# A morphological dilation with seven row sides in PSUM, their ends merged into the pair tiles

## The reference, cut to what matters

```python
pad = jnp.pad(u, ((0, 0), (0, 0), (r, r), (r, r)), constant_values=NEG)   # r = 5
def body(acc, idx):                       # idx = 0 .. 120: 11 rows di x 11 columns dj
    sl = dynamic_slice(pad, (0, 0, di, dj), (Bn, C, H, W))
    acc = maximum(acc, sl - kflat[:, idx][None, :, None, None])
```

## Time and profile before

| what | value |
|---|---|
| median of 3 runs (lowest to highest) | 10253.23 us (10250.52 to 10257.87) |
| the profiled execution: its time, and its span in the trace | 10254.56 us, 10252.8 us |
| DVE, ACT, POOL, PE busy over the span | 97%, 90%, 87%, 84% |
| DMA issued by POOL (queue q0), share of the 16 engines | 60.9% |

### The profile page before, as it was taken

The page is one execution under the profiler, slowest core; times in us unless marked ns, Lnnn a source line. Parts: engine busy times, 40 slices in busy tenths (PEclk is TensorE's granted clock), DMA queues, the critical chain, the costliest instruction groups (busy, mean ns, idle before and its releaser), DMA issues. The chain is left out here.

```text
span 10252.8 us, 72623 instructions
## 1 busy us (share of the span) xinstructions
PE 8565.8 (84%) x18068; PEld 3322.9 (32%) x18068; DVE 9963.9 (97%) x5623; ACT 9179.9 (90%) x6861; POOL 8875.6 (87%) x3274
## 2 busy tenths in 40 slices
PE   2888888888888888888888888888888887998899
PEld 0333333333333333333333333333333333443333
DVE  8999999999999999999999999999999999999999
ACT  2999999999999999999999999999999997888776
POOL 2889888898988999898988888898889887777998
PEclk9999999999999999999999999999999999999999
DMA  8788878888888888888888888888888876444776
GB/s 322 149 157 151 155 155 159 158 160 158 159 157 159 159 158 159 153 159 156 160 155 156 159 158 160 159 158 157 160 159 158 158 141 137 178 182 187 268 282 258
DMA packets 442070, 1751.43 MB, mean 171 GB/s; under 512 B 23888, under 2 KB 130384, under 8 KB 392784
## 3 DMA queue, kind: packets, MB, share of 16 engines
q0 software_dynamic: 278528, 1110.51, 60.9%
q1 hardware_dynamic: 163152, 636.41, 16.6%
HBM read 391.58 MB, written 201.33 MB: 58 GB/s over the span
## 5 line engine op out<-in xcount | busy, mean ns | idle before, releaser
L589 PE MATMUL chain<-dx,mats 128*128 128x512 f32 x10240 | 4979.5, 632 | 940.6 <-ACT chain L639 940.3
L530 POOL TENSOR_TENSOR m<-m,u 128x2048 f32<-128x2048 f32 x1024 | 4338.1, 4350 | 187.1 <-ACT m L621 185.9
L589 PEld LDWEIGHTS chain<-dx,mats 128*128 128x128 f32 x10240 | 1917.0, 197 | 4002.9 <-ACT chain L639 2095.8
L718 DVE SCALAR_TENSOR_TENSOR acc_a<-m,kt,acc_a 128x2048 f32<-128x2048 f32 x1344 | 3162.5, 2353 | 38.2 <-issue 2.4
L639 ACT ACTIVATE chain<-chain,gap_r 128x1024 f32<-128x1024 f32 x2560 | 2694.2, 1086 | 232.2 <-PE chain L589 230.5
L718 DVE SCALAR_TENSOR_TENSOR acc_a<-t,kt,acc_a 128x2048 f32<-128x2048 f32 x1024 | 2411.9, 2355 | 34.2
L501 POOL DMA_DIRECT2D t<-u x1024 | 1486.4, 1563 | 652.8 <-ACT t L621 635.1
L526 POOL TENSOR_TENSOR m<-u,m 128x2048 f32<-128x2048 f32 x384 | 1707.1, 4445 | 0.0
L621 ACT ACTIVATE t<-dx,gap_l 128x2048 f32<-128x2048 f32 x768 | 1540.5, 2006 | 0.4 <-issue 0.4
L589 PE MATMUL chain<-u,mats 128*128 128x512 f32 x3072 | 1456.0, 605 | 71.8 <-ACT chain L639 71.8
L718 DVE SCALAR_TENSOR_TENSOR acc_a<-u,kt,acc_a 128x2048 f32<-128x2048 f32 x576 | 1357.0, 2356 | 20.5
(11 more groups left out here) (149 smaller groups left out, 6876.4 us busy)
## 6 DMA issues: line engine op xcount, KB each, us to landing
t<-u POOLq DMA_DIRECT2D x1024, 1059.0 KB, 8.7
u<-x_dram SPq DMA_DIRECT2D x32, 2688.0 KB, 30.6
xt<-x_dram SPq DMA_DIRECT2D x32, 2048.0 KB, 14.2
x_scratch<-x SPq DMA_DIRECT2D x64, 1024.0 KB, 10.7
h_scratch<-h SPq DMA_DIRECT2D x32, 2048.0 KB, 7.2
both<-h_scratch SPq DMA_DIRECT2D x64, 1024.0 KB, 9.3
out_dram<-res SPq DMA_DIRECT2D x64, 1024.0 KB, 4.9
both<-x_scratch SPq DMA_DIRECT2D x28, 2304.0 KB, 12.6
```

The lines of the kernel that those rows point to most:

```text
L530: nc.gpsimd.tensor_tensor(m_tile(j), m_tile(j), rows, ALU.add).then_inc(m_ready, 1)
L589: added = nc.tensor.matmul(chain[h][:, r:r + 2, :], weight, src[:, top:top + 2, dj:dj + W], start=False, stop=True, skip_group_check=True)
L718: nc.vector.scalar_tensor_tensor(out=acc_a[:], in0=src, scalar=k_base, in1=acc_a[:], op0=ALU.subtract, op1=ALU.max).then_inc(a_done, 1)
```

## The change

Seven row sides are folded in PSUM instead of six. The five right ones of the old list stop a step earlier (4 instead of 5), and the two taps left over become a pair; the new seventh side has 5 steps. So the steps stay at 29 for each half, and the ends that VectorE reads rise from 12 to 14 halves. A finished half is no longer merged into a second accumulator but into half of a pair tile that waits for its own merge (`chain_targets`: the second `m` or `t` tile behind it in the DVE order), with a scalar that is the difference of the two weights (`k_gap`, 28 columns made once). `acc_b`, its start on ACT and the join are gone. POOL makes 23 pairs instead of 22, eight by clamp instead of six, in 5 tiles instead of 4; 16 pairs stay on DMA; 7 singles stay of 10. The SBUF that POOL's DMAs use as scratch is 8192 bytes a partition, where no size was given before. The four orders are new.

```diff
-CHAINS = ((0, "left"), (1, "right"), (2, "right"), (3, "right"), (4, "right"), (5, "right"))
-NPOOL, NDMA = 16, 16
-CLAMPED = (1, 5, 9, 12, 16, 20)
-MP, TP = 4, 4
+CHAINS = ((0, "left", 4), (1, "right", 4), (2, "right", 4), (3, "right", 4), (4, "right", 4), (5, "right", 4), (6, "right", 5))
+NPOOL, NDMA = 23, 16
+CLAMPED = (3, 4, 6, 10, 12, 14, 15, 18)
+MP, TP = 5, 4
+ACT_ORDER = "xx01r01x01r0r10x101x0u10r1x0r10r10x10r1r01x01x0101r010x10r10x1x0r10r10x10r1x01x01x01r01r01"
+PE_ORDER = "0101010101010101010101010101010101010101010101010101010101"
+DVE_ORDER = "s0y1mmmsyy0m1smmmmy01ymysym01mmmmys0m1ymmyys01ymmymymy01symm"
+POOL_ORDER = "iictittticcittttticcitttticticttititicdittiiittdt"
...
         elif side == "right":
             pairs += [(di, 1, 0), (di, 3, 2)]
-            singles += [(di, 4)]
+            if links == 4:
+                pairs += [(di, 5, 4)]
+            else:
+                singles += [(di, 4)]
...
+def chain_targets():
+    targets = {}
+    order = list(numbered(DVE_ORDER))
+    for place, (kind, ch) in enumerate(order):
+        if kind in "01":
+            tiles = [x for x in order[place + 1:] if x[0] in "my"]
+            targets[int(kind), ch] = tiles[:2][-1]
+    return targets
...
-        acc_b = sb("acc_b", [P, CR, W])
+        k_gap = sb("k_gap", [P, GROUPS, 2 * NCHAIN])
...
-                def start_b(c, s, k):
-                    ...
+                for g in range(GROUPS):
+                    for (h, ch), tile in targets.items():
+                        ...
+                        nc.vector.tensor_tensor(k_gap[:, g, 2 * ch + h:2 * ch + h + 1], kt[:, g, last:last + 1],
+                                                kt[:, g, other:other + 1], ALU.subtract).then_inc(k_gap_ready, 1)
+                dve.wait_ge(k_gap_ready, GROUPS * 2 * NCHAIN)
...
                 def merge_chain(c, h, ch):
-                    part = acc_b[:, h * HR:(h + 1) * HR, :]
+                    tile = targets[h, ch]
+                    part = tile_of(*tile)[:, h * HR:(h + 1) * HR, :]
                     dve.wait_ge(chain_added[h], c * NSTEP + (last_step[ch] + 1))
-                    dve.wait_ge(chain_taken[h], at(c, NCHAIN, ch))
+                    tile_ready(c, *tile)
+                    if ch > 0 and targets[h, ch - 1] == tile:
+                        dve.wait_ge(chain_taken[h], at(c, NCHAIN, ch))
...
                 def merge(c, s, k, kind, j):
...
+                        for h in range(2):
+                            taken = [ch for (half, ch), tile in targets.items() if half == h and tile == (kind, j)]
+                            if taken:
+                                dve.wait_ge(chain_taken[h], at(c, NCHAIN, max(taken) + 1))
...
-                def join(c, s, k):
+                def finish(c, s, k):
+                    dve.wait_ge(x1_squared, c + 1)
                     dve.wait_ge(a_done, at(c, NA, NA))
-                    for h in range(2):
-                        dve.wait_ge(chain_taken[h], at(c, NCHAIN, NCHAIN))
-                    nc.vector.tensor_tensor(acc_a[:], acc_a[:], acc_b[:], ALU.max).then_inc(merged, 1)
...
-    nc = bacc.Bacc("TRN2", target_bir_lowering=False, num_devices=1)
+    nc = bacc.Bacc("TRN2", target_bir_lowering=False, num_devices=1,
+                   dynamic_dma_scratch_size=8192)
```

More of the change, by code:

```diff
@@ L77, in dilation_taps @@
     pairs, singles = [], []
+    sides = {di: (side, links) for di, side, links in CHAINS}
     for di in range(KS):
-        side = dict(CHAINS).get(di)
+        side, links = sides.get(di, (None, 0))
         if side == "left":
@@ L87, in dilation_taps @@
             singles += [(di, 10)]
-    while len(pairs) > NPOOL + len(CLAMPED) + NDMA:
+    while len(pairs) > NPOOL + NDMA:
         di, base, outer = pairs.pop()
@@ L362, in dilation @@
     D_TURNS = POOL_ORDER.count("d")
-    pool_pairs, dma_pairs, (init_b, *singles) = dilation_taps()
-    NPAIR = NPOOL + len(CLAMPED)
+    pool_pairs, dma_pairs, singles = dilation_taps()
+    targets = chain_targets()
+    NPAIR = NPOOL
     relu_pairs = [j for j in range(NPAIR) if j not in CLAMPED]
@@ L378, in dilation @@
     chain_steps = []
-    for ch, (di, side) in enumerate(CHAINS):
-        bases = range(1, 5) if side == "left" else range(9, 4, -1)
+    for ch, (di, side, links) in enumerate(CHAINS):
+        bases = range(1, 1 + links) if side == "left" else range(9, 9 - links, -1)
         chain_steps += [(ch, step, base) for step, base in enumerate(bases)]
@@ L418, in dilation @@
         chain_taken = [sem(f"chain_taken{h}") for h in range(2)]
[L419 removed]
+        k_gap_ready = sem("k_gap_ready")
         a_done = sem("a_done")
[L421 removed]
         joined = sem("joined")
@@ L429, in m_tile, with tile_of, tile_col @@
             return m_tiles[j % MP][:, :, first:first + W]
+        def tile_of(kind, j):
+            return m_tile(j) if kind == "m" else t[j % TP][:, :, 0:W]
+        def tile_col(kind, j):
+            di, base, outer = pool_pairs[j] if kind == "m" else dma_pairs[j]
+            return col(di, outer if kind == "m" and j in CLAMPED else base)
         def at(c, per_chunk, count):
@@ L577, in add_step @@
                     ch, step, base = chain_steps[i]
-                    di, side = CHAINS[ch]
+                    di, side, _ = CHAINS[ch]
                     pe.wait_ge(chain_relu[h], c * NSTEP + (i + 1))
@@ L676, in _ @@
                 nc.vector.memset(x1[:], 0.0).then_inc(pads_set, 1)
+                for g in range(GROUPS):
+                    for (h, ch), tile in targets.items():
+                        last = col(CHAINS[ch][0], chain_steps[last_step[ch]][2])
+                        other = tile_col(*tile)
+                        nc.vector.tensor_tensor(k_gap[:, g, 2 * ch + h:2 * ch + h + 1], kt[:, g, last:last + 1],
+                                                kt[:, g, other:other + 1], ALU.subtract).then_inc(k_gap_ready, 1)
+                dve.wait_ge(k_gap_ready, GROUPS * 2 * NCHAIN)
                 dve.sem_inc(a_done, NA)
-                dve.sem_inc(merged, 1)
                 dve.sem_inc(joined, 1)
@@ L681, in _, with tile_ready @@
                     dve.sem_inc(chain_taken[h], NCHAIN)
+                def tile_ready(c, kind, j):
+                    if kind == "m":
+                        dve.wait_ge(m_ready, c * NPAIR + (j + 1))
+                    else:
+                        dve.wait_ge(t_added[j % TP], c * (len(range(j % TP, NDMA, TP)) * 16) + (j // TP + 1) * 16)
                 def merge_chain(c, h, ch):
-                    di, side = CHAINS[ch]
-                    base = col(di, chain_steps[last_step[ch]][2])
@@ L693, in merge_chain @@
+                    if ch > 0 and targets[h, ch - 1] == tile:
+                        dve.wait_ge(chain_taken[h], at(c, NCHAIN, ch))
+                    nc.vector.scalar_tensor_tensor(out=part, in0=chain[h][:],
+                                                   scalar=k_gap[:, g, 2 * ch + h:2 * ch + h + 1], in1=part,
                                                    op0=ALU.subtract, op1=ALU.max).then_inc(chain_taken[h], 1)
                 def merge(c, s, k, kind, j):
[L696 to L706, removed]
-                    else:
-                        di, base = singles[j]
-                        src = u[s][:, k * CR + di:k * CR + di + CR, base:base + W]
@@ L711, in merge @@
+                    k_base = kt[:, g, at_col:at_col + 1]
                     done = a_after[kind, j]
@@ L747, in _ @@
                                         merge(c, s, k, kind, j)
-                                join(c, s, k)
+                                finish(c, s, k)
 def load_resampled(sp, x1_pl, h_pl, hw, xw, hw_loaded, xw_loaded, n, what):
```

19 lines of the change are left out of this document (5 added, 14 removed).

## The result

The changed kernel takes 10369.99 us (median of 4 runs, 10368.8 to 10372.44) where the kernel before took 10251.93 beside it (10250.52 to 10257.87): 1.0115 of its time, 95% interval 1.01 to 1.013. It is slower by 118 us; the forecast was 10162 and the range ended at 10280. The profiled execution took 10368.8 us.

A forecast was written before the change was run, and what follows sets the result against it. A ring of waits through PE, ACT, POOL, DMAs and DVE was taken as the bound: 14.9 + 54.1 + 39.2 + 22.6 = 130.8 us a chunk, 1.45 less, times 64 = 93 us, giving 10162 us; range 10070 to 10280.

The forecast's parts named there:

- DVE's stream: VectorE's own instructions in a chunk: 128.0 us after the change, 2.8 less than before.
- POOL's work: One pair and two clamps more, 7.6 us a chunk: 125.8 busy, still under 128.0, spare time down from 14 to 2.
- `k_gap` and scratch at nothing: The 28 subtractions before the first chunk (7.8 us) and the smaller DMA scratch were both taken to cost nothing.
- The ring: Waits from side 0's half merge through PE, ACT, POOL, DMAs and DVE, closing once a chunk: 130.8 us, chance 0.50.
- Legs 1 to 3: From DVE's half merge `1` of side 0 to the landing of `i14`: 14.9, 54.1 and 39.2 us.
- leg 3: Transfers `i9` to `i14` one behind the other: five of 6.1 us and a landing of 8.7, 39.2 us.
- leg 4: DVE from merge `y14` through the chunk's end to letter `1` of the next chunk: 22.6 us.
- The 1.4 us that DVE lost before: DVE's old loss per chunk, mostly halves not ready; not added, as taken to lie within the 2.8 us it waits.
- The slower rival: Transfers sharing the DMA engines take 6.7 us each, period 134.4, 10392 us; slower by any cause had chance 0.16.
- The third rival: No change: POOL without pauses runs pairs at 3.88 us instead of 3.76, period 132.1, 10245 us; chance 0.12.
- leg 2: POOL from pair `t5` to issue `i9`: 11 pairs, 4 issues and 4 clamps, 54.1 us.
- The first rival: DVE stays the bound because DMAs overlap more or a wait is slack: period 129.4, 10072 us; chance 0.22.

The follow-up runs named there:

- the last kernel: The changed kernel with POOL's string written anew and ACT's and DVE's strings fitted to it: 10100.54 us, 0.9851 of the kernel before.
- the last two: The changed kernel with POOL's string written anew (10117.46 us, 0.9871), and the same with ACT's and DVE's strings also refitted (10100.54 us, 0.9851).

## Why the prediction was wrong, point by point

- **DVE's stream, right.** 128.0 us a chunk; with 6.1 of waits it gives the measured 134.1. The halves merged into pair tiles keep their price.
- **POOL's work, right in size, wrong in what follows.** 125.8 a chunk, as summed. "POOL busy near 125.8 a chunk and its waits for ACT nearly gone" was half wrong: it waits 8.3 us a chunk and is still not on time, since its waits lie mostly ahead of `i15`, `t1` and `i2`, and from `t1` to `i10` it has none. The work added at `i15` shows that it was not too full.
- **`k_gap` and scratch at nothing, right.** The first chunk's last line starts 3.8 us earlier than before (347.0 for 350.8), so the subtractions delay nothing that shows, and the scratch alone did nothing.
- **The ring, right in kind, wrong in its path and in one term.** Legs 1 to 3 were sized within 1.5 us each and 0.3 together, and the transfers of leg 3 did run one behind the other. The step that failed is leg 4: "DVE merges `y14` and goes through the rest of the chunk to letter `1` of the next one", 22.6 us. It took 26.2. The sum counted DVE's instructions there and no wait, although both halves of side 6 and half `0` of the next side 0 stand in it and need PE; DVE waits 3.6 us there. And it was not `y14` that DVE waited for, as the prediction had it ("`y14` first"), but `y10`, 2.04 us in the mean and in every chunk: the ring that set the period is the one by `i10`, `y10`, side 6 and `t1`.
- **What hid that term.** "The 1.4 us that DVE lost before are not added, since they now lie in the 2.8 that it waits anyhow." Waits lie in one another only if they are in the same place of the chunk. A `t` tile that is late in front of side 5 makes the halves of side 6 and of the next side 0 later, so these waits follow one another, and they cannot be taken as part of the wait ahead of `y14`. "The tightest ring that I find" was one of two that share POOL's queue; the other, by `y10` and the row sides, was not summed. The string of DVE shows it: whatever stands ahead of a half delays the next side.
- **The slower rival.** Its 10392 is near the measured 10370, and its mechanism, each transfer at 6.7 us, is not what ran: from `i9` to `i14` they land 6.0 us apart, not 6.7, and the same transfers, issued in another order, gave 10239.67 and 10117.46. Queueing is a part, 1.2 us at `i10`. Its sign, a median landing far above 8.7 with a period above 132.25, did come (11.5 and 134.15), but much of that landing is POOL's own record (last section). The time fell near that rival's by luck. The third rival, slower pairs, did not come either: leg 2 took 52.7, not more than 54.1.
- **The first rival**, DVE as the bound with a period of 129.4 and 10072 us, is near what the same instructions reach in another order: 129.97 and 10100.54 in the last kernel. What a new order would give the kernel before was not tried; with DVE's own 130.8 of its 132.25 us it has less than 1.5 us a chunk to win with the same instructions.
- **What stays open.** How much of the 43.9 us from `y10` back to `t1` is TensorE's lower clock. PE's 16 matmuls behind each pause take 8.57 and 8.84 us, where two groups of 8 take 2 x 3.71 and 0.2 between them, 7.6; that is 1.0 and 1.2 us more, in stretches where the granted clock falls (last section). Whether this lengthens the ring was read from rows only, as part of the 3.0 us that ACT waits for PE on that way; no run kept PE busy through a pause. The clock alone does not order the kernels: in the runs its mean is 0.969 before and 0.972 after, where the time rose. But it is higher in the faster ones (0.979 with `i9` and `i10` earlier, 0.986 and 0.985 in the last two), so a part of their gain may be the clock's. The kernel with `i9` and `i10` earlier still has such a stretch, one side later (0.77 over 9 us, behind a pause of 5.39).

## What to carry to other kernels

Where several in-order engines are each near full, the time is set by rings through their queues, and a ring is summed by walking every instruction that stands between two letters, with the waits of the other rings added wherever they fall in a different place. Work taken off the busiest engine is then worth what the order of the others lets through: here the same instructions ran in 10370 and in 10101 us. To find whether an instruction is on the ring, put a small amount of harmless work ahead of it and the same amount elsewhere, and expect less than that amount where a queue on the ring takes some of it up; and do not add up the gains of two edits that were measured one at a time.

## What the hardware showed that was not expected

**TensorE's clock falls in pauses of a ring.** The windows of the kernel after around the two pauses above (length, busy us of PE, PEld, DVE, ACT, POOL, then the granted clock):

```profile
4055.00:4070.00 15.00, 13.14 (x30) 5.00 (x29) 12.87 (x7) 14.79 (x12) 15.00 (x8) 1.00 1.03 180
...
4074.00:4083.00 9.00, 7.89 (x15) 3.53 (x16) 8.89 (x5) 7.92 (x6) 5.89 (x3) 0.81 1.00 177
...
4098.00:4107.00 9.00, 8.79 (x16) 3.46 (x16) 8.76 (x5) 7.56 (x6) 8.59 (x6) 0.81 0.82 144
```

The clock was full (2.4 GHz) in the first stretch. PE then stood still for 3.71 us, and the mean granted clock of the next 9 us was 0.81, so part of it ran at 1.2 GHz: 0.50, the 1.2 GHz level, in the first 2 us in which PE ran again (4075 to 4077), 1.00 from 4079 on. Behind the second pause, of 2.13 us, it was 0.81 too. The Trainium skill's "TensorE: Matmul & The Clock Gate", in its section on HAM oscillation, tells of bursts that start at the lower clock after each wait; the trace agrees, with that 0.50. Over the whole dilation the granted clock is 0.97, as before.

**A record of POOL starts before the one ahead of it has ended.** `i10`'s record in the fence above lasts 3.67 us where an issue costs 1.25, and `t16`'s before it 6.28 where a pair costs 3.76: `t16`'s ends at 4058.60, 2.51 us behind the start of `i10`'s. So the length of a record is not the price of its instruction. The page's landing of the `t` transfers, counted from the record's start:

```profile
DMA to landing us min/median/max: 8.1/11.5/16.6
```

The median rose from 8.7 to 11.5. In the mean it rose by 1.5 us, 0.9 of it the issue's own record (1.56 to 2.44) and 0.6 behind its end. From the record's end a transfer alone lands 7.0 us later in both kernels. Two whose records end 5 us apart, as those of `i9` and `i10`, land 6.0 us apart in this chunk and 6.2 in the mean, near the 6.1 that the prediction took for each.
